# 32-row blocks of a triangular inverse made on VectorE, in a gated-delta-net layer

## The reference

```python
def step(Sst, inp):
    q_t, k_t, v_t, a_t, b_t = inp
    Sst = Sst * a_t[..., None, None]
    kv = jnp.einsum('bhd,bhde->bhe', k_t, Sst)
    delta = (v_t - kv) * b_t[..., None]
    Sst = Sst + jnp.einsum('bhd,bhe->bhde', k_t, delta)
    o_t = jnp.einsum('bhd,bhde->bhe', q_t, Sst) * scale
    return (Sst, o_t)
_, o = jax.lax.scan(step, S0, (qs, ks_, vs, als, bts))
o = rms_norm(o) * o_norm_w * jax.nn.silu(gate)
h = o.reshape(b, s, H * DV) @ Wo
x = x + h
y = jnp.square(jax.nn.relu(rms_norm(x) @ W_fc)) @ W_proj
```

## Time and profile before

| what | value |
|---|---|
| median of 3 runs | 2603.5 us (2597.47 to 2603.93) |
| the profiled execution | 2604.09 us |
| its span, first to last instruction | 2602.2 us |
| TensorE matmul busy | 2436.9 us, 94% |
| VectorE busy | 1643.2 us, 63% |
| ScalarE busy | 1125.7 us, 43% |
| GpSimd busy | 922.9 us, 35% |
| mean granted TensorE clock | 0.965 |

### The profile page before, as it was taken

How to read it: one execution, slowest core, us unless ns; L and a number is a source line. 1 busy time by engine, 2 the same in 40 slices (tenths; PEclk the granted TensorE clock), 3 DMA queues, 4 the chain that set the end, 5 groups by cost and what they waited for, 6 DMA issues and landing times.

```text
span 2602.2 us, 53235 instructions
## 1 busy us (share of the span) xinstructions
PE 2436.9 (94%) x16411; PEld 2208.2 (85%) x16411; DVE 1643.2 (63%) x3875; ACT 1125.7 (43%) x2351; POOL 922.9 (35%) x2106
## 2 busy tenths in 40 slices
PE   4599999999999999999999999977679999999998
PEld 4488899999989989989989899865569989999887
DVE  6456665666666666666666666547757666766554
ACT  2343343344344344434334334335555555555443
POOL 0133344344344344334334434300034434344432
PEclk9899999999999999999999999885689999999999
DMA  5301111110111111111111111259844445454441
GB/s 180 95 21 34 27 29 23 34 32 22 34 30 24 32 32 24 32 32 25 32 27 29 23 34 29 62 184 299 290 152 157 176 156 170 148 179 158 134 130 21
DMA packets 229961, 218.16 MB, mean 84 GB/s; under 512 B 130028, under 2 KB 204144, under 8 KB 220688
## 3 DMA queue, kind: packets, MB, share of 16 engines
q1 hardware_dynamic: 177360, 185.63, 22.7%
q0 software_dynamic: 11280, 29.31, 3.9%
q10 hardware_dynamic: 41264, 2.51, 1.0%
HBM read 164.65 MB, written 54.53 MB: 84 GB/s over the span
## 4 chain that ended last, share of the span: by engine, by line
PE 87%; DVE 5%; DMA 2%; issue 2%; SPq 1%; ACT 1%; ACTq 0%; POOL 0%; DVEq 0%; POOLq 0%
PE ps_front L765 13%; PE ps_back L1950 11%; PE ps_inva L765 8%; PE ps_invb L765 8%; PE ps_back L765 8%; PE ps_back L2011 5%; PE ps_back L1994 4%; PE ps_invb L1933 4%; PE ps_inva L1916 4%; PE ps_front L1896 4%; PE ps_back L2019 4%; PE ps_invb L1944 2%; PE ps_front L1889 2%; PE ps_invb L1935 1%; PE ps_inva L1918 1%
## 5 line engine op out<-in xcount | busy, mean ns | idle before, releaser
L628 DVE TENSOR_TENSOR w_lo<-w_raw,w_hi 128x512 fp32r<-128x512 f32 x288 | 189.8, 687 | 4.0 <-ACT w_hi L717 0.2
L765 PE MATMUL ps_back<-w_hi,eh_hi 128*128 128x256 f32 x624 | 180.1, 289 | 3.2 <-DVE eh_lo L638 3.2
L1224 POOL TENSOR_SCALAR xrow_v<-bag 128x1 f32<-128x1 f32 x31 | 7.1, 228 | 495.9 <-DVE bag L1741 495.9
L765 PE MATMUL ps_back<-w_hi,eh_lo 128*128 128x256 f32 x624 | 176.4, 283 | 0.0
L765 PE MATMUL ps_back<-w_lo,eh_hi 128*128 128x256 f32 x624 | 176.4, 283 | 0.0
L717 ACT ACTIVATE w_hi<-w_raw 128x512 fp32r<-128x512 f32 x288 | 169.6, 626 | 0.0
L1728 DVE TENSOR_TENSOR oT<-oT 128x512 f32<-128x512 f32 x64 | 44.3, 692 | 171.6 <-ACT oT L1385 171.6
L729 ACT ACTIVATE sact<-ps_inva 128x512 f32<-128x512 f32 (+1 forms) x96 | 49.8, 519 | 236.0 <-PE ps_inva L765 236.0
L1368 ACT ACTIVATE yi<-ps_invb 128x512 f32<-128x512 f32 x128 | 71.2, 624 | 183.4 <-PE ps_invb L1944 183.3
L1950 PE MATMUL ps_back<-state,kqT_t 128*128 128x128 f32 x1024 | 134.3, 286 | 11.0 <-DVE la L1752 11.0
L765 PE MATMUL ps_inva<-xT_hi,w_hi 128*128 128x512 f32 (+1 forms) x384 | 135.2, 352 | 1.7 <-DVE xT_lo L633 1.7
(11 more groups left out here) (392 smaller groups left out, 7191.5 us busy)
## 6 DMA issues: line engine op xcount, KB each, us to landing
w_raw<-wts_d SPq DMA_DIRECT2D x72, 1024.0 KB, 5.0
wts_d<-prep SPq DMA_DIRECT2D x96, 256.0 KB, 3.9
dT<-alphaT_d SPq DMA_DIRECT2D x32, 512.0 KB, 3.8
prep<-L_ffn_W_gate_dram SPq DMA_DIRECT2D x32, 256.0 KB, 3.3
prep<-L_ffn_W_up_dram SPq DMA_DIRECT2D x32, 256.0 KB, 3.8
prep<-L_ffn_W_down_dram SPq DMA_DIRECT2D x32, 256.0 KB, 4.6
x_all<-L_attn_x_dram SPq DMA_DIRECT2D x4, 1024.0 KB, 9.7
hTr<-hT_d SPq DMA_DIRECT2D x32, 128.0 KB, 2.0
```

The source lines that it names most:

```text
L628: V.tensor_tensor(piece(w_lo[p], m).bitcast(F32R), piece(w_raw, m), piece(w_hi[p], m), ALU.subtract).then_inc(split[n], 1)
L765: ins = MM(out_, w[a].bitcast(F32R), x[b].bitcast(F32R), start=start and n == 0, stop=stop and n == 2)
```

## The change

`L0` goes from 4 to 5, so TensorE's first level is gone: 2 levels, 5 and 6, remain, and all counts of semaphores follow. The 32x32 diagonal blocks are instead completed on VectorE. For each pair of 16x16 blocks X11, X22 with the block L21 below the diagonal, `pair_products` makes W = X22 x L21 and `pair_inverse` makes X21 = W x X11, on 128 lanes: 32 pairs (4 per head, 8 heads), four rows of the block in each of four lanes. Each is one product over 1024 elements and one sum of 16, then a small transposing copy.

What that takes in DMAs per step: four stores `low_d` and one load `pair_a` for L21, two loads `pair_x2` and `pair_y1` from `xy_d`, one store `x21_d` and four stores `y21_d` (pieces of 16 bytes), four loads into `x4` and four into `y4`, all on SP. The working tiles lie in `xi`, `yi`, so they have to wait for the levels and `state_u` of tile t. The lanes are ordered anew (`lanes_of`), odd blocks in the upper half. ScalarE's `copy_x` waits for 12 loads and for the `y21_d` stores, before the silu of projection 3.

Every engine's `step` has a new order. Some constants' semaphores are merged and the small loads come first in the program.

```diff
-L0, LEVELS = 4, 7
+L0, LEVELS = 5, 7
+            def pair_products(f):
+                dve.wait_ge(pair_loaded, 16 * 3 * f + 16 * 3)
+                if not (isinstance(f, int) and f == 0):
+                    for g in range(G):
+                        u = BU_U + g
+                        dve.wait_ge(back_filled[u % 2], b_filled(f - 1, u))
+                ch = Chain(dve, lane_dve, (N_LANE + N_PAIR) * f + N_LANE)
+                ch.link(V.tensor_tensor(pair_p, pair_cube(pair_rows(pair_x2, QW), 2), pair_cube(pair_rows(pair_a, W16), 1), ALU.mult))
+                ch.link(V.tensor_reduce(pair_rows(pair_w, QW), pair_p, X, ALU.add))
+            def pair_inverse(f):
+                rows = pair_rows
+                ch = Chain(dve, lane_dve, (N_LANE + N_PAIR) * f + N_LANE + N_PAIR // 2)
+                ch.link(V.tensor_tensor(pair_p, pair_cube(rows(pair_w, QW), 2), pair_cube(rows(pair_y1, W16), 1), ALU.mult))
+                ch.link(V.tensor_reduce(rows(pair_x, QW), pair_p, X, ALU.add))
+                V.tensor_copy(rows(pair_y, W16), rows(pair_x, QW).rearrange("p a n -> p n a")).then_inc(pair_ready, 1)
```

SP, in `blocks_to_lanes`, `lanes_to_blocks` and the new `pairs_to_blocks`:

```diff
-                if more:
-                    load_alpha(f + 1)
                 sp.wait_ge(lt_stored, 16 * NB16 * f + 16 * NB16)
                 sp.dma_start(lane_l[:, 0:W16 * W16], lt_d[:, :]).then_inc(lt_loaded, 16)
+                for m in range(NB32):
+                    sp.dma_start(low_d[...], aP[...]).then_inc(low_stored, 16)
+                if more:
+                    load_alpha(f + 1)
+                    ... wait for both level_t of tile t ...
+                sp.wait_ge(low_stored, 16 * NB32 * f + 16 * NB32)
+                sp.dma_start(pair_a, ...).then_inc(pair_loaded, 16)
                 sp.wait_ge(xy_stored, 16 * f + 16)
+                sp.dma_start(pair_x2, ...).then_inc(pair_loaded, 16)
+                sp.dma_start(pair_y1, ...).then_inc(pair_loaded, 16)
+            def pairs_to_blocks(f):
+                sp.wait_ge(pair_ready, f + 1)
+                sp.dma_start(x21_d..., pair_x).then_inc(x21_stored, 16)
+                for n in range(4):
+                    sp.dma_start(y21_d..., pair_y[l, :]...).then_inc(y21_stored, 16)
+                sp.wait_ge(x21_stored, 16 * f + 16)
+                for m in range(NB32):
+                    sp.dma_start(x4[...], x21_d[...]).then_inc(x4_loaded, 16)
+                sp.wait_ge(y21_stored, 16 * 4 * f + 16 * 4)
+                for m in range(NB32):
+                    sp.dma_start(y4[...], y21_d[...]).then_inc(y4_loaded, 16)
```

More of the change, by code:

```diff
@@ L1086, in step @@
                 if before:
-                    tail(t - 1)
+                    tail_x1(t - 1)
                 sp.dma_start(xin[:, 0, :], x_tiles[t]).then_inc(xin_loaded, 16)
+                if more:
+                    pairs_to_blocks(f)
+                if before:
+                    tail_xf(t - 1)
             load_hT(0)
@@ L1265, in step @@
                 gate(t)
+                if more:
+                    decayed_k(f, q)
                 if tail:
@@ L1462, in step @@
                     tail_x(t - 1)
-                if more:
-                    blocks_y(f)
-                if ahead:
-                    silu(f + 1, 2, False)
             hT_high(0, 0)
@@ L1755, in step @@
                 f, q = t + 1, 1 - p
-                state_in(t, p)
-                level_t(t, L0)
                 if more:
                     k_sum(f)
-                level_x(t, L0)
+                state_in(t, p)
+                if tail:
+                    tail_xln(t - 1)
+                    tail_o(t - 1)
+                if more:
+                    decay_products(f)
+                    delta_scalars(f, q, False)
+                    for n in range(4):
+                        delta_products(f, q, n)
+                level_t(t, L0)
+                if tail:
+                    tail_x2(t - 1)
                 if ahead:
@@ L1763, in step @@
                     V.tensor_tensor(hT_lo[:, p].bitcast(F32R), hTr[:, :, :], hT_hi[:, p], ALU.subtract).then_inc(h_split, 1)
-                if tail:
-                    tail_o(t - 1)
-                    tail_xln(t - 1)
-                if more:
-                    decay_products(f)
-                level_t(t, L0 + 1)
-                if tail:
-                    tail_x2(t - 1)
-                level_x(t, L0 + 1)
-                if more:
-                    delta_scalars(f, q, False)
-                    for n in range(4):
-                        delta_products(f, q, n)
+                level_x(t, L0)
                 if tail:
@@ L1783, in step @@
                 if more:
-                    lanes(f)
+                    pair_products(f)
                 if tail:
@@ L1801, in _ @@
             lanes(0)
+            pair_products(0), pair_inverse(0)
             step(0, 0, True, True, False)
```

222 lines of the change are left out of this document (130 added, 92 removed).

## The result

The changed kernel takes 2891.5 us (median of 4 runs, 2890.1 to 2899.9) beside 2602.9 for the kernel before on the same chip: a ratio of 1.112, 95% interval 1.109 to 1.115. That is slower by 11%. The direction and the mechanism were those of the forecast, the size was not: 2821 had been forecast, and the range ended at 2885, 6.5 us under the measured time.

A forecast was written before the change was run, and what follows sets the result against it. TensorE set the pace before; afterwards a chain through all engines was to take 56.8 us a step against 49.57. 29 such steps give +210, first and last steps +7: 2604+217 = 2821 us, range 2670 to 2885.

The forecast's parts named there:

- item 5: Behind the lanes: 2.7 us from xy_d store to next issue, two loads landing in 2.0; 28.2, pair_products to 30.7 us.
- the clock: Rival: TensorE's clock falls after gaps ahead of delta_products 2 and tail_proj, 1.5 to 2.8 us a step; 2880 us, 13%.
- Items 1 to 3: Step's head: products and tail_wo to 6.2 us, hT_lo to 7.7, lt_d stores from 8.3, lane_l load at 13.1.
- Item 4: VectorE's lanes meet GpSimd's scaled_v, price 0 to 1.9 us; real work starts at 16.7 and ends at 22.9.
- Items 6 and 7: tail_x1 to 32.3 us, x_root beside pair_inverse to 37.5 (0.9 lost), then tail_xf and square_sums to 39.3.
- Item 8: GpSimd's o_roots and k_root behind square_sums: 14.8 us, giving nbh at 54.1, now what the products wait for.
- Item 9: VectorE's delta_scalars held by GpSimd's gate, bounds 0 and 2.4 us, taken as 2.4; the chain closes at 56.8.
- a free port: Rival: the port is free when delta_scalars comes, so no hold-up by gate; step of 54.4 us, 2750 us, 22%.
- the long loop: The forecast itself: the chain through all engines closes at 56.8 us against 49.57; 2821 us, 2785 to 2855, 40%.
- The cover: ScalarE's copy_x, behind the y21_d stores and x4 loads, may start at 44 us and stays hidden, 5 us ahead.
- The rival on the other side: TensorE stays the bound: the other engines' chain fits into its 46.1 us step; 2510 us, 12% with smaller gains.
- The count: Some 29 steps repeat, each longer by 56.8-49.57 us: +210 us; first and last steps together about +7.

The follow-up runs named there:

- sp_order: Changed kernel with SyncE's wait for hT_lo and next hT load moved behind the stores of the lower blocks: 2790.3 us, ratio 1.071.
- gate_late: Changed kernel with GpSimd's decayed_k put ahead of gate, so gate no longer runs while dbh starts: 2807.5 us, ratio 1.079.
- two_extra_products: Changed kernel with the first product of the pair stage made three times instead of once: 3011.8 us, ratio 1.157.
- y1_later: both_orders with the pair_y1 load on its own semaphore, awaited by pair_inverse instead of pair_products: 2625.7 us, ratio 1.010.
- lanes_outer: Changed kernel with pair lanes numbered 4 x lane + quarter, so the pair transfers' outermost dimension is 32 or 128, not 4: 2877.2 us, ratio 1.104.
- both_orders: Changed kernel with the edits of sp_order and gate_late together: 2697.5 us, ratio 1.036.
- all_four: both_orders with the edit of y1_later and with square_sums ahead of tail_xf on VectorE: 2578.1 us, ratio 0.990.
- loads_alone: Changed kernel with the sixteen diagonal-block loads into x and y moved later on the SyncE and ScalarE queues: 2888.3 us, ratio 1.108.

## Why the prediction came out as it did

The step that failed is item 5, the landing of the two pair loads, with the clock, which the sum had left out, behind it. In offsets from the zero of the step shown, with the forecast first:

- **Items 1 to 3 held.** `tail_wo` ends at 6.2 / 6.4, `hT_lo` at 7.7 / 7.6, the stores start at 8.3 / 8.5, the lanes' load is issued at 13.1 / 13.3. `sp_order` showed that the wait for `hT_lo` is on the loop.
- **Item 4 held**, with the mechanism: the opening copy took 1.13 us beside `scaled_v` and ended with it; the lanes end at 22.9 / 22.7.
- **Item 5 failed**: the pair products start at 28.2 / 29.95. I took the landing of both loads from the like-sized `hTr` (2.0). A size doesn't make two transfers alike: VectorE started 4.1 us after the issue of the broadcast one, and it landed in 2.6 when its dimensions were turned. From the end of the lanes to the pair products I had 5.3 us; it is 7.2 in the step shown and 7.1 in the usual one, so the term was 1.8 us a step too small, 54 us in all.
- **Items 6 and 7** close at 39.3 / 40.9, the 1.6 us carried over; a GpSimd instruction took 0.99 us in place of 0.27, so 0.7 was lost where 0.9 was counted. The product of 1024 elements, estimated at 1.2, took 1.23.
- **Item 8**: 14.8 / 15.6, in the usual step 15.0. In the one shown VectorE waited for the logits, and `k_sum` and `k_root` behind them came later; I had not counted that.
- **Item 9 held to the point**: 2.32 us, and `gate_late` removed it alone. So the 22% for a free port were misplaced. The rule weighed in the prediction (the Trainium skill, "SBUF — State Buffer", "Who interferes with whom") agrees with 0.17 against 2.32 us, for an instruction of only 8 columns. The first of the two rows that I named for it doesn't belong to it: the opening copy of the lanes reads one SBUF tensor, not two. It was held all the same, and the product behind it, which reads two, would have met `scaled_v` in its place, so item 4 keeps its price.
- **The cover held**: `copy_x` starts at 44 / 45.7.
- **The clock is a term, not a rival.** I had set it at 13% against the long loop; both came. The gap that I forecast ahead of `delta_products` 2 was 4.6 us; it was 3.1 in the mean, and between 560 and 1560 us the clock fell in the steps in which it was 4.0 or more. At full clock a step takes 58.2; 9 of the 30 took 59.7 to 61.3, and the mean is 58.93. That is 0.7 x 30 = 21 us. The rival on the other side, TensorE as the bound, fell with `two_extra_products`.
- **The count**: 30 periods lie between the first and the last `dbh` of the steady loop, not 29, one times 7.2.

Together: 54 us for the loads, 21 for the clock, 7 for the count, less some 12 us of small terms (0.4 a step: the lanes ended 0.2 earlier, from `nbh` to the next zero it is 2.3 us and not 2.7, and item 8 took 0.2 more), which is 70, and 70 were missed. The separate shares are read from traces; that the loads are a cause was shown by `y1_later` and `lanes_outer`. That the clock is one rests on steps of one kernel that do the same work, and no run held it fixed.

The rest of the question, where the removed level went: it was saved, but on an engine that had stopped being the bound. Some 194 of the 289 us lost were two places in the new order (`both_orders`), and a further 119 one more place and one wait (`all_four`); with these, the same blocks and the same second trip are 24 us faster than the kernel before.

## What to carry to other kernels

When work moves off the busiest engine into a round trip, draw the loop that goes through all engines from one step to the next and count every piece that stands on it, instructions of 0.2 us too: what they wait for costs their neighbour's length. After each edit read the waits again before the next one is placed; a gap that was free in one trace was gone in the next. And count TensorE's clock as a term of the loop as soon as a gap opens ahead of it: a saving made elsewhere in the loop can be paid back there almost in full (`lanes_outer`), and one that shortens the gap itself gains more than its own length (`gate_late`).

## What the runs showed of the hardware

- A broadcast load of 128 KB from device memory with its four copies as the outermost dimension (changed kernel): VectorE started 4.1 us after its issue. With the copies inside (`lanes_outer`) it was 2.6 to 2.7 us. The packets took 2.0 us with 3.8 at once, against 0.8 us with 8.4. The page of the profile gave no landing time for the first kind.
- Four stores of 512 pieces of 16 bytes each landed in 3.0 us each, issued every 0.66 us (changed kernel; the last landed 5.6 us after the first was issued, by the median, where I had estimated 6).
- TensorE's clock: behind 4.05 us of idle eight matmuls took 3.78 us, behind 3.16 us 3.38, behind 2.78 us 1.99. The granted clock over the 8 us around the first was 0.59, so most of them ran at 1.2 GHz and not 2.4. The length of the gap alone doesn't decide it. In `loads_alone` one of 3.90 us cost nothing:
```profile
1036.31 1.99 PE L1976 MATMUL ps_front<-kqT_t 128*128 128x256 f32 x8 [3.90 <-DVE aP L1658]
```
- A GpSimd product beside VectorE instructions that read PSUM and one SBUF tensor cost neither anything (`gate_late`: 2.36 us, and 1.74 for four). Beside one that reads two SBUF tensors it cost that one 2.1 us (changed kernel: 2.32 for 0.17).
